# A graph layer on one core: part of the next tile's one-hots written ahead of the wait for a tile's sum, and gather landings counted in three blocks

## The chip, the core and the metric

The kernel runs on one core of a Trainium2 chip, as one program. The time is the device time of that core in microseconds, the median of several runs. The profile is of one execution; its own time stands beside its span, since the durations quoted come from it.

Engines are named as the profile names them: PE is TensorE's matmuls (PEld its weight loads), DVE VectorE, ACT ScalarE, POOL GpSimd, SP SyncE. DVEq, ACTq and so on are the sequencers of these engines, where register work and DMA issues run.

## What is computed

The input `x` has 6250 rows of 256. It is layer-normalised, then three things are added to it: a graph layer, a gated linear-attention layer, and after a second normalisation a feed-forward layer that acts on the half of the rows with the largest routing weight.

```python
h_sparse = _maxk(h_neigh, 32)                  # xn @ W_neigh, largest 32 of each row
msg = h_sparse[src]                            # 200000 edges, dst sorted
summed = jax.ops.segment_sum(msg, dst, num_segments=n)
neigh = summed / jnp.maximum(deg, 1.0)[:, None]
x = x + xn @ W_self + neigh + mix(xn)
x = x + ffn(layernorm(x))                      # for the rows that the router picks
```

The edges are sorted by destination, and low destinations have many more edges than high ones.

## The kernel before, in words

The rows are cut into 50 tiles of 125. A first part (to about 365 us) computes the sparse rows, split into two half-precision parts, and stores them in DRAM as `rows_d` (1 KB a row), and the statistics of the attention. The second part, about 77% of the time, is a hardware loop of five iterations with ten tiles (*positions* `s` = 0 to 9) unrolled in each. Tile `n = 10 i + s` is called by its number from 0 to 49 below.

**The sum of a tile.** Sorted edges are cut into groups of 512 (4 chunks of 128). For each group POOL issues four indirect gathers into `ring`, a ring of 8 groups (L600). SP waits for their landing, and counts it for PE in `s_landed` (L504). DVE writes the group's one-hot matrices (128 edges by 125 rows, four of them in one instruction, L1306) into `onehot`, a ring of `HOT` = 8 groups. PE multiplies: four matmuls of one-hot by rows (L954) and four small ones for the degree (L955). One such step on either engine is a *visit*. The last visit of a tile stands apart from the loops, since its group is shared with the next tile and isn't released. The limits of a tile, `g0` and `g1`, depend on the data: they are in the table `bounds` in SBUF, and each engine reads them into registers (`load`, L400), one tile ahead, at the end of the tile before (`look_ahead`).

**The dense tiles.** The five tiles with the most edges are not gathered. Their edges are counted by (source row, destination) in *windows*: DVE writes one-hots of pairs of chunks (L1331, L1337), PE multiplies them (L926), ACT copies the counts out (L726). Windows stand in positions 0 to 6 (`SHARE`: two in each of 0 to 5, one in 6). In positions 7 to 9 PE multiplies the counts with all rows of `rows_d`, in eight *pieces* (`from_rows`, L994). The pieces are loaded by ACT's queue (`load_h`, L696) into two buffers `hs`, 750 or 875 KB each; the first two when the last window has been copied out, each later one when PE has used the piece two before it. Position 9 has no gathered groups.

**The order inside a tile.** On PE: `ffn_down` (L905) and `ffn_up` (L898) of earlier tiles, `mix_hidden` (L864, which waits for DVE's `s_mix` of the tile before), `project`, `mix_open`, in positions 7 to 9 one piece, then `gathered`: the groups `g0` to `g1` cut into quarters or halves by `cut`, and between the cuts `turn_x3` (L890, the transpose of `x3`) and the windows or further pieces. The last matmul (L1031) signals `s_agg`. On DVE: the one-hots of visits and windows in the same order (`gathered`), then the rows of the attention and feed-forward results (L1382 to L1298), then the wait for `s_agg` (it ends at L1390), then the chain from the sum to `x2`, its normalisation, `x3` and the router weight (L1390 to L1433), each step waiting for the one before it. In ACT's stream the copy of the transposed `x3` (L684, it waits for `turn_x3`) stands ahead of the loads of the pieces.

All waits are on semaphores that count up. `s_step` is a set of 21 semaphores, one for each step of DVE's chain.

## Time and profile before

| | us |
|---|---|
| median of 3 runs | 2132.38 (2130.95 to 2132.94) |
| the profiled execution's own time | 2125.73 |
| its span | 2124.0, mean granted TensorE clock 0.854 |
| PE busy | 1572.6 (74% of the span) |
| DVE busy | 1250.0 (59%) |
| POOL busy | 1200.1 (57%) |
| ACT busy | 438.4 (21%) |

Busy shares are averages over stages with different limits. The waits and the order in time in the rows further below say which engine is waited for, and where.

### The profile page before, as it was taken

What the parts mean: (1) busy time and instruction counts of PE and PEld (TensorE: products, weight loads), DVE (VectorE), ACT (ScalarE), POOL (GpSimd) and SP (SyncE); (2) the same over time, 40 slices, a digit from 0 to 9 for tenths busy, and PEclk for the clock granted to TensorE, in tenths of its full rate; (3) what the DMA queues carried; (4) which work ended last, traced back from release to release, by engine and by line L of the source; (5) the groups of instructions that cost most, each with busy time, mean ns of one, the idle gap of its engine ahead of it and who ended that gap; (6) DMA issues with size and microseconds to landing.
All of it is one profiled execution on the core that took longest, in us unless ns stands there. A gap on an engine that the chain in (4) does not pass through costs nothing. (4 is left out here: it accounts for less than half of the span.)

```text
span 2124.0 us, 40110 instructions
## 1 busy us (share of the span) xinstructions
PE 1572.6 (74%) x8607; PEld 1132.7 (53%) x8608; DVE 1250.0 (59%) x3823; ACT 438.4 (21%) x974; POOL 1200.1 (57%) x1348
## 2 busy tenths in 40 slices
PE   2398554788778578888768888868898778887740
PEld 0154353355455456656656666656666566665630
DVE  5599973877566324666533766525666326663452
ACT  0254231011111112122112222112222122222200
POOL 1054544767777776777774777654676526664000
PEclk7699776888889788899987988889989889998865
DMA  4222114333343553334453433453333533335233
GB/s 134 75 84 72 58 45 127 90 95 108 108 118 110 153 178 110 110 109 118 139 175 111 116 104 113 143 153 87 92 111 109 158 100 106 96 96 149 68 107 117
DMA packets 149369, 236.37 MB, mean 111 GB/s; under 512 B 24807, under 2 KB 113859, under 8 KB 149219
## 3 DMA queue, kind: packets, MB, share of 16 engines
q0 software_dynamic: 52480, 142.82, 23.7%
q10 hardware_dynamic: 63586, 59.79, 9.3%
q1 hardware_dynamic: 33153, 31.95, 4.7%
q8 instruction: 71, 1.16, 0.2%
q14 instruction: 79, 0.65, 0.1%
HBM read 208.46 MB, written 26.01 MB: 110 GB/s over the span
## 5 line engine op out<-in xcount | busy, mean ns | idle before, releaser
L600 POOL DMA_INDIRECT ring<-rows_d,stage x1088 | 1075.8, 989 | 551.9 <-issue 303.6
L954 PE MATMUL bank<-ring,region_v 128*125 x1260 | 450.8, 469 | 90.5 <-SPq L504 45.3
L1306 DVE SCALAR_TENSOR_TENSOR region_v<-iota,tile_start,dstT 128x500 f16 x315 | 233.6, 742 | 189.5 <-issue 179.7
L954 PEld LDWEIGHTS bank<-ring,region_v 128*125 x1260 | 198.2, 157 | 241.2 <-issue 178.7
L926 PE MATMUL bank<-region_k 128*125 x622 | 214.4, 433 | 88.2 <-DVE region_k L1337 47.8
L1337 DVE TENSOR_SCALAR region_k<-iota,win_start,region_k 128x500 f16 x622 | 231.9, 414 | 1.2 <-issue 1.2
L905 PE MATMUL bank<-region_v 128*125 128x256 f32 x848 | 216.8, 413 | 16.6 <-issue 16.3
L955 PE MATMUL bank<-ones,region_v 128*125 128x2 f16 x1260 | 222.6, 177 | 0.0
L955 PEld LDWEIGHTS bank<-ones,region_v 128*125 x1260 | 201.3, 160 | 3.1 <-issue 2.5
L898 PEld LDWEIGHTS bank<-region_v 128*128 128x128 f32 x1664 | 196.6, 194 | 2.8
L1390 DVE TENSOR_SCALAR col_deg<-bank 125x1 f32<-125x1 f32 x50 | 7.9, 158 | 322.0 <-PE bank L1031 322.0
L898 PE MATMUL bank<-region_v 128*128 128x125 f32 x1664 | 196.8, 277 | 0.0
L905 PEld LDWEIGHTS bank<-region_v 128*125 128x125 f32 x848 | 170.1, 206 | 45.3 <-issue 17.1
L926 PEld LDWEIGHTS bank<-region_k 128*125 x622 | 85.0, 142 | 191.8 <-issue 185.0
L1331 DVE SCALAR_TENSOR_TENSOR region_k<-iota,region_k 128x250 f16 x311 | 131.4, 422 | 92.1 <-issue 66.1
L994 PE MATMUL bank<-region_k 125*125 125x512 f16 x250 | 84.4, 489 | 105.0 <-DMA region_k<-rows_d 105.0
L690 ACT ACTIVATE region_v<-bank,b 128x125 f32<-128x125 f32 x416 | 112.2, 381 | 113.3 <-PE bank L898 89.3
L726 ACT ACTIVATE region_k<-bank 125x500 f16<-125x500 f32 (+1 forms) x65 | 37.6, 579 | 381.9 <-PE bank L941 381.9
L690 ACT ACT_TABLE_LOAD x51 | 65.4, 1283 | 223.1 <-PE bank L905 137.4
L994 PEld LDWEIGHTS bank<-region_k 125*125 125x125 f16 x250 | 40.7, 174 | 130.5 <-DMA region_k<-rows_d 108.5
L573 POOL CAST region_r<-region_r 125x256 f16<-125x256 f32 x50 | 20.0, 399 | 150.9 <-DVE region_r L1210 149.3
L677 ACT ACT_TABLE_LOAD x51 | 65.4, 1283 | 188.3 <-PE bank L994 150.4
(284 smaller groups left out, 1968.3 us busy)
## 6 DMA issues: line engine op xcount, KB each, us to landing
region_k<-rows_d ACTq DMA_DIRECT2D x30, 750.0 KB
ring<-rows_d,stage POOLq DMA_INDIRECT x1088
region_k<-rows_d ACTq DMA_DIRECT2D x10, 875.0 KB
region_v<-xT_d ACTq DMA_DIRECT2D x53, 125.0 KB, 5.0
xT_d<-region_r ACTq DMA_DIRECT2D x51, 125.0 KB, 2.1
region_v<-in_x_dram SPq DMA_DIRECT2D x5, 1250.0 KB
rows_d<-region_r SPq DMA_DIRECT2D x50, 125.0 KB
region_k<-in_x_dram ACTq DMA_DIRECT2D x50, 125.0 KB
```

Source lines behind the costliest of these rows:

```text
L600: pool.indirect_dma_start(out=ring[:, c, :], out_offset=None, in_=rows_d, in_offset=bass.IndirectOffsetOnAxis(ap=stage[:, c:c + 1], axis=0 ...
L677: act.activation(hgT[0:GH, :], hg_pre, ACT.Gelu, bias=bg1[:, 0:1]).then_inc(s_hg, 1)
L690: last = act.activation(hidT[:, n, :], bank[(7, 4)[n // 4]][:, n % 4 * T:(n % 4 + 1) * T], ACT.Gelu_apprx_tanh, bias=b1[:, n:n + 1])
L898: m = pe.matmul(bank[(7, 4)[n // 4]][:, n % 4 * T:(n % 4 + 1) * T], w1[:, k, n * 128:(n + 1) * 128], x3T[:, k, :], start=(k == 0), stop=(k ...
L905: m = pe.matmul(out, hidT[:, n, :], w2[:, n, :], start=(n == 0), stop=(n == NH - 1))
L926: m = pe.matmul(out, lo_words[:, u * LW:(u + PAIR * (HOT_PAIRS - 1)) * LW + T][:, bass.ds(lo, T)], key_words[:, u * KEYS:(u + PAIR * (HOT_ ...
L954: m = pe.matmul(total, onehot_s, row_s, start=False, stop=False, skip_group_check=True)
L955: d = pe.matmul(deg_sum, onehot_s, ones16[:], start=False, stop=False, skip_group_check=True)
L994: m = pe.matmul(dense_sum, counts16[:, b, :], hs[:, q % 2, (b - first) * 2 * C:(b - first + 1) * 2 * C], start=False, stop=False, skip_gro ...
L1306: dve.scalar_tensor_tensor(out=hot_slots[:, bass.ds(hot, GC), :], in0=iota[:, 0:T].rearrange("p (a t) -> p a t", a=1).to_broadcast([128, G ...
L1331: dve.scalar_tensor_tensor(out=lo_hot[:, bass.ds(slot, PAIR), :], in0=iota[:, 0:T].rearrange("p (a t) -> p a t", a=1).to_broadcast([128, P ...
L1337: last = dve.tensor_scalar(key_words[:, u * KEYS:(u + PAIR * (HOT_PAIRS - 1) + 1) * KEYS][:, bass.ds(key, KEYS)], iota[:, 0:KEYS], win_fla ...
```

## The change

There are three parts. First, the first `LEAD` = 4 groups of a tile (or all up to `g1`, if there are fewer) get a limit of their own, `led`, in a new part of the table (`T_LEAD`). DVE writes their one-hots in the tile before, between the feed-forward rows and the wait for `s_agg` (`hot_ahead`). It does so for the first tile ahead of the loop, and not in position 8, since position 9 has no groups. On PE the visits of these groups come first, then `turn_x3`, and only then the rest; `cut` now cuts `led` to `g1`, without the first quarter, and the window or piece of each section comes ahead of its visits and not behind them. Second, `look_ahead` reads two values (`T_G1` and `T_LEAD`) where it read one, and on DVE it comes ahead of the wait. Third, the landings are counted in three sets of semaphores for blocks of 20, 20 and 10 passes over the edges (`s_land[block][q]`), and the steps of DVE's chain in 7 semaphores with three counts each. With the data of this run there is one pass: only block 0 runs, and the other two are jumped over behind it.

```diff
-    def __init__(self, engine, semaphores, count):
+    def __init__(self, engine, semaphores, counts):
     def mark(self, instruction):
-        instruction.then_inc(self.semaphores[self.n], 1)
+        instruction.then_inc(self.semaphores[self.n // len(self.counts)], 1)
+    def at(self, n):
+        return self.semaphores[n // len(self.counts)], self.counts[n % len(self.counts)]
...
     HOT = 8
+    LEAD = HOT // 2
+    BLOCKS = ((0, 20), (20, 20), (40, 10))
...
             def look_ahead(self, n, last):
                 if not last:
                     self.ahead = load(self.engine, n + 1 + T_G1)
+                    self.lead = load(self.engine, n + 1 + T_LEAD)
...
         def cut(engine, g0, g1, parts):
-            if not parts:
+            if parts < 2:
                 return [g0, g1]
             middle = engine.snap((g0 + g1) // 2)
-            first = [engine.snap((g0 + middle) // 2)] if parts > 1 else []
             last = [engine.snap((middle + g1) // 2)] if parts > 2 else []
-            return [g0] + first + [middle] + last + [g1]
+            return [g0, middle] + last + [g1]
```

On PE:

```diff
-                    cuts = cut(pe, g0, g1, len(parts) + len(sums))
+                    with pe.If(led > g0):
+                        with pe.Fori(g0, led) as g:
+                            visit(finals, g, True, total)
+                    if turn:
+                        turn_x3(one)
+                    cuts = cut(pe, led, g1, len(parts) + len(sums))
                     for at, (first, end) in enumerate(zip(cuts, cuts[1:])):
-                        with pe.If(end > first):
-                            with pe.Fori(first, end) as g:
-                                visit(finals, g, True, total)
-                        if turn and at == 0:
-                            turn_x3(one)
                         if at < len(parts):
                             count_window(i, *parts[at])
                         elif at < len(sums):
                             from_rows(sums[at])
+                        with pe.If(end > first):
+                            with pe.Fori(first, end) as g:
+                                visit(finals, g, True, total)
                     visit(finals, g1, False, total)
```

On DVE:

```diff
+            def hot_ahead(n, i, s):
+                if s == PER - 1:
+                    first, finals = load(dve, n + (T_G0 + 1)), load(dve, n + (T_VIS + 1))
+                    led = load(dve, n + (T_LEAD + 1))
+                else:
+                    first, finals, led = ends.end, ends.visits + (s + 1), ends.lead
+                with dve.If(led > first):
+                    with dve.Fori(first, led) as g:
+                        visit(finals, g, tile_after(i, s, 1))
...
-                    cuts = cut(dve, g0, g1, len(parts))
+                    cuts = cut(dve, led if s < PER - 1 else g0, g1, len(parts))
                     for at, (first, end) in enumerate(zip(cuts, cuts[1:])):
+                        if at < len(parts):
+                            window(i, *parts[at])
                         with dve.If(end > first):
                             with dve.Fori(first, end) as g:
                                 visit(finals, g, tile)
-                        if at < len(parts):
-                            window(i, *parts[at])
                     visit(finals, g1, tile)
...
-                st = Places(dve, s_step, one)
+                st = Places(dve, s_step, [dve.snap(n * 3 + u) for u in (1, 2, 3)])
...
                 ffn_rows(st, n, y_sum, yw[:, u, :], one)
+                ends.look_ahead(n, s == PER - 1)
+                if s != PER - 2:
+                    hot_ahead(n, i, s)
                 dve.wait_ge(s_agg, one)
...
-                st.after(a)
-                ends.look_ahead(n, s == PER - 1)
+                if s + 1 < PER and SHARE[s + 1] == 0:
+                    hold(dve, *st.at(a))
+                else:
+                    st.after(a)
```

In the first part of the program, where the table is made, and on SP (POOL's loops are changed in the same way):

```diff
+            dve.memset(bounds[:, T_LEAD + NT:T_LEAD + NT + 1], 0)
+            a = st.mark(dve.tensor_scalar(lead[:], bounds[:, T_G0:T_G0 + NT], float(LEAD), None, ALU.add))
+            st.after(a)
+            dve.tensor_tensor(bounds[:, T_LEAD:T_LEAD + NT], lead[:], bounds[:, T_G1:T_G1 + NT], ALU.min).then_inc(s_bounds, 1)
...
+            def landings(block, passes):
+                with sp.Fori(0, passes) as r:
+                    with sp.Fori(0, rounds) as j:
+                        for q in range(RING):
+                            sp.wait_ge(s_land[block][q], (r * ROUNDS + j + 1) * (16 * GC))
+                            sp.sem_inc(s_landed, 1)
+                            sp.sem_inc(s_restage, 1)
+
+            landings(0, passes)
+            with sp.If(general > 0):
+                for block in range(1, len(BLOCKS)):
+                    landings(block, BLOCKS[block][1])
```

**DVE, around its wait for the tile's sum (position 1).** L1306 is the last one-hot of the tile, L1382 to L1298 are the attention and feed-forward rows, and L1390 is the first instruction behind the wait for `s_agg`. Before:

```order
L1306 SCALAR_TENSOR_TENSOR region_v<-iota,tile_start,dstT 128x500
L1381 REGISTER_ALU
L1382 TENSOR_TENSOR region_k<-region_k,region_v 125x256
L1386 TENSOR_TENSOR region_k<-region_k,bank 125x256
L1296 TENSOR_TENSOR region_v<-bank,region_v 125x256
L1298 ISA
L1298 TENSOR_SCALAR region_v<-region_v,w_at 125x256
L1390 TENSOR_SCALAR col_deg<-bank 125x1
L1391 COPY region_v<-bank 125x256
```

After, L1334 is what was L1298 and L1444 what was L1390. These rows stand between the two; L408 is the reading of table values into registers, L1342 the one-hots of a group:

```order
L408 TENSOR_LOAD bounds
L408 ISA x3
L408 TENSOR_LOAD bounds
L408 ISA x2
L1404 COMPARE_AND_BRANCH
L1405 UNCONDITIONAL_BRANCH
L1405 ISA
L1342 ISA x3
L1342 SCALAR_TENSOR_TENSOR region_v<-iota,tile_start,dstT 128x500
L1405 REGISTER_ALU
L1405 COMPARE_AND_BRANCH
L1404 UNCONDITIONAL_BRANCH
```

Behind the wait there were no one-hots of groups until the chain was done; now up to four stand ahead of it, with two register loads in front.

**PE, at the end of a tile (position 1).** L1031 is the matmul that signals the tile's sum, L905 and L898 are the feed-forward matmuls that follow. Before:

```order
L1030 MATMUL bank<-zeros 125x2
L1031 MATMUL bank<-zeros 125x2
L400 ISA
L400 TENSOR_LOAD bounds
L400 ISA x2
L905 MATMUL bank<-region_v 125x256 x8
```

After, with L1061 for L1031, L932 for L905 and L925 for L898:

```order
L1060 MATMUL bank<-zeros 125x2
L1061 MATMUL bank<-zeros 125x2
L408 ISA
L408 TENSOR_LOAD bounds
L408 ISA x3
L408 TENSOR_LOAD bounds
L408 ISA x2
L932 MATMUL bank<-region_v 125x256 x8
```

A second register load now stands between the end of one tile and the first matmul of the next.

## Rows read from the trace of the kernel before

**Rows 1.** The longest waits of the whole execution: who waits for whom, total, times, longest.

```profile
DVE col_deg L1390 <- PE bank L1031: 322.0, 50, 25.2
...
PE bank L994 <- DMA region_k<-rows_d: 105.0, 14, 10.5
...
PE bank L926 <- DVE region_k L1337: 47.8, 102, 0.8
PE bank L954 <- SPq L504: 45.3, 17, 6.2
...
PE bank L954 <- DVE region_v L1306: 26.9, 50, 1.0
```

**Rows 2.** Timeline of DVE, sum of tile 21 to sum of tile 22: start, us, instruction [idle before, releaser].

```profile
1213.36 0.41 DVE L1290 SCALAR_TENSOR_TENSOR region_v<-region_v,bank 128x250 f32<-128x250 f32 x1
...
1218.82 0.20 DVE L1433 TENSOR_SCALAR w_at<-col_w,br 125x1 f32 x1
1220.98 0.74 DVE L1306 SCALAR_TENSOR_TENSOR region_v<-iota,tile_start,dstT 128x500 f16 x1 [1.96 <-issue]
1222.49 0.42 DVE L1331 SCALAR_TENSOR_TENSOR region_k<-iota,region_k 128x250 f16 x1 [0.77 <-issue]
...
1227.65 0.74 DVE L1306 SCALAR_TENSOR_TENSOR region_v<-iota,tile_start,dstT 128x500 f16 x1 [0.43 <-issue]
...
1236.29 1.60 DVE L1306 SCALAR_TENSOR_TENSOR region_v<-iota,tile_start,dstT 128x500 f16 x2 [0.27 <-issue]
...
1239.28 0.35 DVE L1298 TENSOR_SCALAR region_v<-region_v,w_at 125x256 f32<-125x256 f32 x1
1242.32 0.16 DVE L1390 TENSOR_SCALAR col_deg<-bank 125x1 f32<-125x1 f32 x1 [2.69 <-PE bank L1031]
```

**Rows 3.** L1390's waits in 1145:1334, 1447:1623 and 1735:1898: total, times.

```profile
  PE bank L1031: 15.6, 7
...
  PE bank L1031: 18.3, 7
...
  PE bank L1031: 13.3, 7
```

**Rows 4.** Register loads of DVE's sequencer, 1147 to 2005: ns min/median/max.

```profile
L400 DVEq TENSOR_LOAD <-bounds x78: 300/306/327, 1157.1 to 1993.4; - x78
```

**Rows 5.** Timeline of PE: the first matmuls behind the sum of tile 21.

```profile
1212.38 0.88 PE L905 MATMUL bank<-region_v 128*125 128x256 f32 x3 [0.16 <-issue]
```

**Rows 6.** Timeline of PE in tile 27 (position 7).

```profile
1354.49 3.69 PE L905 MATMUL bank<-region_v 128*125 128x256 f32 x16
...
1361.68 0.64 PE L864 MATMUL bank<-region_v,wg1g 128*64 128x125 f32 x4
...
1365.44 1.72 PE L994 MATMUL bank<-region_k 125*125 125x512 f16 x7
...
1368.18 0.41 PE L890 MATMUL bank<-ident,region_v 125*128 125x125 f32 x2
1374.86 3.25 PE L994 MATMUL bank<-region_k 125*125 125x512 f16 x7 [6.26 <-DMA region_k<-rows_d]
...
1387.67 2.82 PE L994 MATMUL bank<-region_k 125*125 125x512 f16 x6 [7.56 <-DMA region_k<-rows_d]
...
1396.25 0.20 PE L1030 MATMUL bank<-zeros 128*125 128x2 f16 x1
```

**Rows 7.** Timeline of ACT in tile 28 (position 8).

```profile
1410.24 0.38 ACT L684 ACTIVATE region_v<-bank 128x250 f32<-128x250 f32 x1 [4.41 <-PE bank L890]
1410.39 0.28 ACTq L696 DMA_DIRECT2D region_k<-rows_d  x1
```

**Rows 8.** Timeline of PE, tile 28, the piece loaded there.

```profile
1422.17 2.82 PE L994 MATMUL bank<-region_k 125*125 125x512 f16 x6 [9.61 <-DMA region_k<-rows_d]
```

**Rows 9.** POOL's waits for PE in 366:531 (tiles 0 to 2) and 817:930 (10 to 12).

```profile
POOL ring L600 <- PE bank L954: 31.2, 7, 18.5
...
POOL ring L600 <- PE bank L954: 15.3, 5, 10.7
```

100 lines of the change are left out of this document (56 added, 44 removed).

## The prediction

> **What bounds the kernel now.** I read the list of waits first. The reader is to see there that no engine waits for one thing alone: DVE waits for the sum of a tile at every one of the 50 tiles, 322.0 us in all, and PE waits for DVE in small bites (47.8 us for window one-hots, 26.9 us for those of groups), for SP's count of landings (45.3 us) and for the loaded pieces (105.0 us) [rows 1]. Then I laid the timeline out tile by tile. It shows three kinds of stretches.
>
> In the tiles with windows of the last three iterations PE and DVE are nearly level. DVE is idle at the sum only 15.6, 18.3 and 13.3 us over seven tiles each (position 9 and the six behind it) [rows 3], and PE's bites are spread over the same tiles. One tile shows the cycle: the sum of tile 21 is there at about 1212.2 (PE goes on at 1212.38 [rows 5]), DVE's chain ends with L1433 at 1218.8, the first one-hots of the next tile start at 1220.98 after 1.96 us of register work, the last rows (L1298) at 1239.28, and then DVE waits 2.69 us until 1242.32 [rows 2]. DVE works some 27 of 30 us, PE never sits idle for long, and each waits for the other once in a cycle.
>
> In positions 7 and 8 the pieces pace PE: 6.26 and 7.56 us of waiting in tile 27, 9.61 us in tile 28 [rows 6, 8].
>
> In the first two iterations the gathers pace everything. PE waits for SP there, and POOL loses time only where its ring is full. After the start of the first tile (18.5 us, which stays) that is 31.2 - 18.5 = 12.7 us in tiles 0 to 2; behind position 9 of the first iteration it is 15.3 us, of which one wait is 10.7 [rows 9].
>
> **The change part by part.**
>
> *One-hots ahead, in the window tiles.* No instruction of this work is removed: four visits of DVE move from behind the chain to ahead of the wait. What can be gained is DVE's idle time at the sum, 15.6 + 18.3 + 13.3 = 47.2 us in the last three iterations [rows 3]. It is filled completely, because the moved section is longer than any of these waits: two register loads and the set-up, about 2 us, then four visits at 0.74 + 0.27 us, some 5.8 us in all against a wait of 2.69 in the tile shown and 47.2 / 21 = 2.2 on average [rows 2, 3]. From then on DVE is the bound, and what counts is what the new order costs it. I count the gaps of one tile with six visits. Before: 1.96, 0.77, 0.43, 0.77, 0.43 and twice 0.27, together 4.9 us [rows 2]. After: 1.5 from the chain to the first window (one load, no group), 1.0 from window to window past an empty section, 0.43 and 0.27 to the last two groups, about 1.95 ahead of the leading section and three times 0.27 in it, together 6.0. So a tile costs DVE 1.1 us more. Over 18 tiles that is 20, and 47 - 20 = 27. PE can deliver that: its waits for DVE are 47.8 + 26.9 = 74.7 us over some 35 window tiles, 2.1 a tile or 38 over 18 [rows 1]. In the last iteration the cost eats the wait in single tiles, and what one tile has over isn't carried on; I take 3 off. Term: **-24**.
>
> The second load is the disputed price. A load takes 0.306 us on DVE's sequencer [rows 4]; with the operations around it I take 0.7 us, because a section with a load starts 0.77 us after a group's one-hots and one without 0.43 us, while most of the load runs beside the 0.74 us instruction ahead of it [rows 2]. The Trainium skill (DMA: Bandwidth & Descriptors, "Latency and other measured facts") gives a floor of about 600 ns for a `tensor_load`; the trace has half of that, and the trace decides. By the page each extra load would cost 0.3 us more, an estimate of 9 us over the tiles of this term and the loads on PE below.
>
> *The late chain.* DVE now reaches the sum up to 5.5 us late in a window tile. The cover is PE's feed-forward work: it starts at 1354.49 and the first matmul that needs the chain (L864, through `s_mix`) at 1361.68, 7.2 us later [rows 6]. The chain's `s_mix` comes about 1.6 us after its start (L1290 ends at 1213.77 [rows 2]), so 5.5 + 1.6 = 7.1: covered, with nothing to spare. I cost it at nothing. With the cover gone every microsecond counts in each tile where it happens. What is late next is `x3`, which PE needs only behind four visits.
>
> *Gathers.* PE releases four ring slots at once at the start of a tile, where it released one to three before a window. That takes away POOL's waits for a slot that is stuck behind a window. I take half of the 12.7 us in tiles 0 to 2 (the next window holds up a slot again) and, in tiles 10 to 12, the 15.3 - 10.7 = 4.6 us; the 10.7 us itself is the time to PE's first visit and stays [rows 9]. As POOL paces PE in both iterations, these pass to the end: **-11**. In those iterations the faster tiles otherwise only wait longer for landings.
>
> *Positions 6 to 8.* This speaks against the change. A visit takes 1.1 us at the full clock (L890 starts at 1368.18, the matmuls of the piece end about 1367.1 [rows 6]). In position 6 four visits instead of two stand ahead of the last window, so the first pieces are loaded 2.2 us later. In position 8 `turn_x3` moves behind three more visits, and ACT issues the load of the next piece right after the copy that waits for it (1410.24, then 1410.39) [rows 7]. PE waits for that load, so it lands 3 x 1.1 = 3.4 us later [rows 8]. Against that, fewer visits are left behind the last piece. In tile 27 the last piece runs from 1387.67 to about 1390.4, then four visits until 1396.25, 5.9 us, the first at half clock (after the wait the seven matmuls of a piece take 3.25 us where they took 1.72) [rows 6]. Two visits are left, about 3.9 us. So position 7 is level (+2.2 - 2.0), and position 8 loses 3.4 - 1.9 = 1.5, a little less with fewer groups. With 2.7 us for tiles 17 and 18 (both move with `turn_x3`; in tiles 7 and 8 the gathers cover it) and 4 for the last three iterations: **+7**.
>
> *PE's second register load.* The first matmul after a tile's sum already starts with a gap of 0.16 us [rows 5], so one load is just hidden behind the last visit and 0.7 us more is not. Where DVE or the gathers pace, this is covered; in positions 6, 8 and 9 of four iterations it isn't: 13 x 0.7, **+9**.
>
> *The rest.* Three short DVE operations and two waits for the table: **+1**. The three blocks of landings cost nothing in a run with one pass: the same waits and gathers run, and the jump over the other blocks comes when POOL has issued its last gather. The seven step semaphores change no order and hold as many waits.
>
> Sum: -24 - 11 + 7 + 9 + 1 = **-18 us**. The profiled execution took 2125.7 us, 6.7 below the median of the runs, so 2107.7 in its terms, and **2114 us** as a median.
>
> **The rivals.**
>
> *More is gained* (chance 0.17). For: the register work of the leading section may start while DVE's last rows run, and PE's load may find cover in the visits that now follow each other without waits. With DVE's extra at nothing (-20) and PE's loads free (-9) the time is 2114 - 29 = 2085; half of it 2099. Against: 1.96 us of exposed register work stands in every tile [rows 2].
>
> *Nothing is left* (0.14). The gathers are as late as before, since the next window holds the slots (+11), and the tiles with five groups gain nothing (+5): 2130. For: in an iteration paced by landings only POOL's own waits can be won, and I could place only half of them.
>
> *DVE's chain comes too late* (0.13, the other side). The place is PE's L864. If the leading section is longer than I think, or holds for a free one-hot slot, PE waits there and the cycle grows by the same amount. At 1.0 us more per tile the 18 tiles give back 18 us and the gain is gone; that is the point from which it decides. At 1.5 us more: +27, so 2141. For: the margin is 0.1 us. Against: the slot that the fourth leading one-hot needs was freed five visits before the end of the tile, and DVE was busy for only part of the cycle.
>
> My forecast has 0.56. It covers 2104 to 2124, and the two neighbours add 2094 below and 2134 above; beyond these I leave 2 in 10. About 0.2%, 4.3 us, is what a measurement of this kernel can tell from no change. Faster by more: the forecast, the larger gain and a third of the nothing-case, with some of the forecast lost, 0.74. Within: 0.13. Slower: 0.13.
>
> **What the profile of the changed kernel would show.** DVE's wait at the sum nearly gone in positions 0 to 5, left in 7 and 8. PE's waits for group one-hots near zero, those for window one-hots no smaller than before, since DVE is the bound. L1061 to L932 on PE 0.8 us apart instead of 0.4. POOL's waits for PE shorter in tiles 0 to 2. The load of the piece in position 8 some 17 us after the sum of the tile before instead of 14, and PE's wait for it as long as before, since PE comes later too. I am wrong if PE waits at `mix_hidden` for DVE, if the window tiles are more than 1.5 us a tile faster, or if POOL's waits are what they were.

## The result, and the profile after

| | before | changed |
|---|---|---|
| median of the runs beside each other | 2130.95 us (7 runs, 2122.79 to 2133.31) | 2144.22 us (7 runs, 2142.09 to 2152.93) |
| profiled execution, its span | 2125.73, 2124.0 us | 2152.93, 2151.2 us |
| mean granted clock of TensorE | 0.854 | 0.836 |

The ratio is 1.0076 [1.0053, 1.0099]: the change costs 0.76%, where a gain of 18 us, 0.8%, was forecast. The profiled execution of the changed kernel is the slowest of its seven and that of the kernel before lies 5 us under its median, so the two traces are 27 us apart and the medians 13. What follows splits up the 27, so about half of it lies in which executions were profiled, and not in the change.

The longest waits of PE in the changed kernel (who waits for whom, total, times, longest), to be read beside [rows 1]:

```profile
PE bank L1024 <- DMA region_k<-rows_d: 124.7, 16, 12.2
PE bank L953 <- issue: 63.5, 203, 0.7
...
PE bank L932 <- issue: 29.9, 15, 5.6
PE bank L981 <- SPq L517: 29.2, 11, 6.7
PE bank L953 <- DVE region_k L1373: 24.1, 57, 1.3
...
PE bank L960 <- ACT region_k L753: 15.0, 14, 1.2
...
PE bank L981 <- DVE region_v L1342: 11.9, 16, 3.7
```

The same view of the kernel before, from a second execution that was profiled among the experiments (before_here):

```profile
PE bank L926 <- DVE region_k L1337: 49.9, 107, 0.8
PE bank L954 <- SPq L504: 45.1, 17, 7.8
PE bank L926 <- issue: 37.7, 115, 0.6
PE bank L954 <- DVE region_v L1306: 28.3, 54, 0.7
...
PE bank L905 <- issue: 19.0, 6, 4.9
...
PE bank L933 <- issue: 9.3, 23, 0.8
```

The reader is to see an exchange of names. As waits for DVE the view has 36.0 us (24.1 + 11.9), not 78.2 (49.9 + 28.3). In return more stands under "issue", PE's own register work, in front of the matmuls of windows (L953, before L926) and of the feed-forward (L932, before L905). And 15.0 us stand at L960, the first matmul of a window (before, L933), which the view puts down to ACT. PE also waits 124.7 us for the pieces, not 105.0.

Such a label needs a second look. The view names whoever signalled last within the gap, also where PE's sequencer was busy with registers meanwhile. PE and ACT in tile 22:

```profile
1241.06 0.21 PE L960 MATMUL bank<-zeros 128*125 128x2 f16 x1 [1.10 <-ACT region_k L753]
```

```profile
1240.03 0.59 ACT L753 ACTIVATE region_k<-bank 125x500 f16<-125x500 f32 x1 [3.09 <-PE bank L968]
```

ACT copies the counts of the window just ended, but by the code the new window waits only for the copy of the one before that. PE's sequencer branches, loads a table value (0.30 us from 1240.31) and works on registers from 1239.8 to 1241.0: these 15 us are PE's own work too. The same holds for most of what is labelled as waiting for DVE. In the kernel before, the matmul at L926 has a gap of 0.33 us on average where the view names nobody (37.7 us, 115 times) and 0.47 where it names DVE (49.9 us, 107 times).

DVE's longest waits in the changed kernel:

```profile
DVE col_deg L1444 <- PE bank L1061: 225.6, 31, 23.1
...
DVE region_v L1342 <- issue: 154.3, 260, 2.7
...
DVE region_k L1433 <- DMA region_k<-in_x_dram: 133.9, 14, 19.8
...
DVE region_k L1367 <- issue: 110.8, 96, 8.6
```

The wait for the sum fell from 322.0 us in 50 tiles to 225.6 in 31 [rows 1]; it is mostly gone in the window tiles, as it was meant to be. One of them, tile 21 to 22, on DVE's timeline (start, us, instruction, idle before):

```profile
1226.49 0.20 DVE L1487 TENSOR_SCALAR w_at<-col_w,br 125x1 f32 x1
1228.07 0.43 DVE L1367 SCALAR_TENSOR_TENSOR region_k<-iota,region_k 128x250 f16 x1 [1.38 <-issue]
...
1233.97 0.42 DVE L1367 SCALAR_TENSOR_TENSOR region_k<-iota,region_k 128x250 f16 x1 [1.21 <-issue]
...
1239.39 1.61 DVE L1342 SCALAR_TENSOR_TENSOR region_v<-iota,tile_start,dstT 128x500 f16 x2 [0.84 <-issue]
...
1242.27 0.35 DVE L1334 TENSOR_SCALAR region_v<-region_v,w_at 125x256 f32<-125x256 f32 x1
1244.69 0.74 DVE L1342 SCALAR_TENSOR_TENSOR region_v<-iota,tile_start,dstT 128x500 f16 x1 [2.06 <-issue]
...
1250.41 0.16 DVE L1444 TENSOR_SCALAR col_deg<-bank 125x1 f32<-125x1 f32 x1 [1.89 <-PE bank L1061]
```

Four one-hots stand between 1244.69 and 1248.5, and DVE still waits 1.89 us for the sum, where it waited 2.69 [rows 2]: the sum itself comes later, 31.7 us behind the one before instead of 30.1. The starts of sections cost 1.38, 1.21, 0.84 and 2.06 us.

Where the time went shows best between two ends of a sum on PE (the last L1031 or L1061 of each tile). Added up by position over the five iterations (tile 0 left out), in us:

| kernel | positions 9 and 0 to 5 | 6 | 7 | 8 | 6 to 8 |
|---|---|---|---|---|---|
| before | 1060 | 141 | 193 | 176 | 510 |
| before_here | 1060 | 140 | 193 | 177 | 511 |
| changed | 1070 | 136 | 214 | 174 | 525 |

The two executions of the kernel before took nearly the same time (2125.73 and 2125.12 us), and their sums agree to 1 us. That isn't the scatter of one kernel: the seven runs of each kernel spread over 11 us. So the 10 us, and the 14 to 15, are those of this one execution of the changed kernel; the experiments below repeat their pattern in other traces. The rest of the 27: the first sum ends 3.4 us later, and half a microsecond comes back behind the last.

*The window tiles.* Four stretches from the sum of tile 8 to that of tile 15, 18 to 25, 28 to 35, 38 to 45. First the second execution of the kernel before, then the changed one (length, busy time of each engine, PE's granted clock, share of DMA, GB/s):

```profile
797.30:1021.00 223.70, 192.94 (x1114) 140.43 (x1114) 146.52 (x420) 47.49 (x103) 162.25 (x172) 0.91 0.39 111
1126.00:1332.60 206.60, 180.25 (x1036) 132.56 (x1036) 130.85 (x381) 47.49 (x103) 133.92 (x142) 0.89 0.37 104
1427.30:1619.80 192.50, 167.59 (x985) 125.66 (x985) 120.25 (x357) 47.49 (x103) 115.30 (x122) 0.90 0.34 99
1715.30:1898.40 183.10, 159.29 (x955) 120.50 (x955) 114.80 (x345) 47.49 (x103) 101.33 (x108) 0.93 0.33 93
```

```profile
798.00:1025.70 227.70, 196.42 (x1114) 142.06 (x1115) 150.44 (x424) 47.44 (x103) 165.24 (x175) 0.88 0.40 113
1127.60:1338.70 211.10, 183.17 (x1036) 135.27 (x1037) 132.48 (x384) 47.45 (x103) 135.16 (x143) 0.86 0.36 103
1438.80:1632.20 193.40, 171.53 (x985) 127.80 (x985) 121.73 (x361) 47.44 (x103) 110.74 (x117) 0.86 0.34 97
1731.50:1919.30 187.80, 163.84 (x954) 124.69 (x953) 116.55 (x349) 47.45 (x103) 95.88 (x101) 0.88 0.31 89
```

The same matmuls keep PE busy 715.0 us instead of 700.1, at a granted clock of 0.86 to 0.88 instead of 0.89 to 0.93. PE's idle time in these stretches, added up by what ended it: 53.1 us for DVE and 51.3 of "issue" before; 17.3 for DVE, 71.8 of "issue" and 15.0 at L960 in the changed kernel. So 36 us less under DVE's name stand against 36 more under the others: PE's idle time is the same, 105 us. How much of it PE really waited shows in the rows of its sequencer: before DVE's signal it had nothing to do for 10.7 of the 53.1 us before, and for 3.6 of the 17.3 after; at L960 for 0.4 of the 15.0. The rest is PE's own register work, before and after. The net loss is the longer busy time at a lower clock.

*Positions 7 and 8.* PE in tile 27 (position 7), then in tile 28, and ACT in tile 28:

```profile
1383.02 3.25 PE L1024 MATMUL bank<-region_k 125*125 125x512 f16 x7 [5.28 <-DMA region_k<-rows_d]
1397.68 2.82 PE L1024 MATMUL bank<-region_k 125*125 125x512 f16 x6 [11.42 <-DMA region_k<-rows_d]
```

```profile
1432.79 2.82 PE L1024 MATMUL bank<-region_k 125*125 125x512 f16 x6 [10.28 <-DMA region_k<-rows_d]
```

```profile
1421.24 0.38 ACT L711 ACTIVATE region_v<-bank 128x250 f32<-128x250 f32 x1 [6.74 <-PE bank L917]
1421.39 0.28 ACTq L723 DMA_DIRECT2D region_k<-rows_d  x1
```

In tile 28 the load goes out 17.2 us after the end of the sum (1404.2), PE waits 10.28 us where it waited 9.61 [rows 8], and the position is level. In tile 27 the piece in the middle starts 23.6 us after the end of the sum (1359.4) where it started 20.4 us after it (1354.5), and the last one costs 11.42 us of waiting where it cost 7.56 [rows 6].

ACT shows why tile 27 loses. Its sequencer issues a store and three small loads between the sum and the load of the middle piece, and the store's issue is long. First before_here (sum at 1353.6), then the changed kernel (1359.4):

```profile
1354.45 9.92 ACTq L739 DMA_DIRECT2D yw_d<-region_v  x1
...
1370.41 0.29 ACTq L696 DMA_DIRECT2D region_k<-rows_d  x1
```

```profile
1361.19 12.00 ACTq L766 DMA_DIRECT2D yw_d<-region_v  x1
...
1379.62 0.29 ACTq L723 DMA_DIRECT2D region_k<-rows_d  x1
```

The store goes out 0.9 us after the sum before and 1.7 with the change, and holds the sequencer 2 us longer. Ahead of it stand the loads of the first two pieces, the second of them issued 5.6 us ahead of the sum before and 2.8 us ahead of it with the change, since four visits now stand ahead of the last window (with two, in lead_2, it is 5.6 again). Tiles 37 and 47 show the same, so the load of the middle piece is late there because the first pieces are.

DVE's wait for the input rows (L1433) grew from 57.1 us in before_here to 133.9, and they come by the same queue. In tile 29 ACT issues a store and then that load, first in before_here, then in the changed kernel:

```profile
1428.22 0.30 ACTq L739 DMA_DIRECT2D yw_d<-region_v  x1
1428.62 0.59 ACTq L716 DMA_DIRECT2D region_k<-in_x_dram  x1
```

```profile
1439.74 5.72 ACTq L766 DMA_DIRECT2D yw_d<-region_v  x1
1445.55 1.32 ACTq L743 DMA_DIRECT2D region_k<-in_x_dram  x1
```

DVE has the rows at 1454.32, builds the next tile's one-hots behind them, and reads the sum of tile 29 at 1462.11, 5.5 us after it was there (1456.6). The four tiles of position 0 behind it took 160 us, where the kernel before has 148 and 152.

### The profile page after: what moved, and what is told of

The parts are those of the page before. It is cut to its first block and busy times, and to the rows that moved or that the text cites. A ratio compares the mean times of both kernels' runs of the same rounds, so it can differ in the third digit from the quotient of the medians.

```text
span 2151.2 us, 40690 instructions
## 1 busy us (share of the span) xinstructions
PE 1585.5 (74%) x8607; PEld 1143.3 (53%) x8608; DVE 1247.0 (58%) x3826; ACT 438.0 (20%) x974; POOL 1199.7 (56%) x1348
## 3 DMA queue, kind: packets, MB, share of 16 engines
q0 software_dynamic: 52480, 142.82, 23.6%
## 5 line engine op out<-in xcount | busy, mean ns | idle before, releaser
L981 PE MATMUL bank<-ring,region_v 128*125 x1260 | 429.9, 460 | 57.5 <-SPq L517 29.2
L1342 DVE SCALAR_TENSOR_TENSOR region_v<-iota,tile_start,dstT 128x500 f16 x315 | 233.8, 742 | 188.4 <-issue 154.3
L953 PE MATMUL bank<-region_k 128*125 x622 | 225.0, 455 | 88.5 <-issue 63.5
L932 PE MATMUL bank<-region_v 128*125 128x256 f32 x848 | 234.0, 437 | 30.0 <-issue 29.9
L932 PEld LDWEIGHTS bank<-region_v 128*125 128x125 f32 x848 | 182.8, 222 | 63.3 <-issue 31.3
L925 PEld LDWEIGHTS bank<-region_v 128*128 128x128 f32 x1664 | 196.2, 194 | 2.8
L925 PE MATMUL bank<-region_v 128*128 128x125 f32 x1664 | 196.4, 277 | 0.0
L953 PEld LDWEIGHTS bank<-region_k 128*125 x622 | 88.1, 145 | 197.9 <-issue 191.5
L1024 PE MATMUL bank<-region_k 125*125 125x512 f16 x250 | 83.9, 487 | 124.8 <-DMA region_k<-rows_d 124.7
L1444 DVE TENSOR_SCALAR col_deg<-bank 125x1 f32<-125x1 f32 x50 | 7.8, 156 | 225.6 <-PE bank L1061 225.6
```

The lines of the kernel that those rows point to most:

```text
L925: m = pe.matmul(bank[(7, 4)[n // 4]][:, n % 4 * T:(n % 4 + 1) * T], w1[:, k, n * 128:(n + 1) * 128], x3T[:, k, :], start=(k == 0), stop=(k ...
L932: m = pe.matmul(out, hidT[:, n, :], w2[:, n, :], start=(n == 0), stop=(n == NH - 1))
L953: m = pe.matmul(out, lo_words[:, u * LW:(u + PAIR * (HOT_PAIRS - 1)) * LW + T][:, bass.ds(lo, T)], key_words[:, u * KEYS:(u + PAIR * (HOT_ ...
L981: m = pe.matmul(total, onehot_s, row_s, start=False, stop=False, skip_group_check=True)
L1024: m = pe.matmul(dense_sum, counts16[:, b, :], hs[:, q % 2, (b - first) * 2 * C:(b - first + 1) * 2 * C], start=False, stop=False, skip_gro ...
L1342: dve.scalar_tensor_tensor(out=hot_slots[:, bass.ds(hot, GC), :], in0=iota[:, 0:T].rearrange("p (a t) -> p a t", a=1).to_broadcast([128, G ...
```

## The experiments

The first eight runs (no_lead to lead_6_8) fell on two chips on which the kernel before itself takes 2675 to 2676 us, not 2130. The last section says what is different there; their ratios aren't carried over to the first chip. The other ten, from before_here on, fell on three chips and ran beside a kernel before of 2126 to 2130 us.

Which positions build ahead, and which keep the order of before, is a table in all of these; the code of a position in OLD is that of the kernel before:

```diff
+    LEADS = (...)   # positions with a leading section
+    OLD = (...)     # positions in the order of the kernel before
...
-                if s != PER - 2:
+                if (s + 1) % PER in LEADS:
                     hot_ahead(n, i, s)
```

**no_lead**, and once more as **no_lead_2**: `LEADS = ()`, `OLD = 0..8`.

> The change without any one-hots ahead: no position has a leading section, and the order of visits, transpose, windows and pieces is that of the kernel before. What stays is the three blocks of landings, the seven step semaphores, the larger table and the second register load of look_ahead, ahead of the wait on DVE. If the cost is in the moved one-hots and the new order, this is within 0.2% of the kernel before. If it is in the added code and loads (the loop is entered 5.7 us later in the changed kernel's trace, and its loads stand at 50 tile ends), it is slower by 6 us or more, 0.3%.

> No one-hot is built ahead and every position has the order of the kernel before; what is left of the change is the three blocks of landings with their own semaphores, the rewritten counts and the loads of one more table. Both theories expect no change, 0.998 to 1.002. More than 1.003 would say that part of the loss comes from the blocks or from where the code lies, and not from the order of the work.

Measured, at 2675 us: 1.0031 [0.9998, 1.0064] and 1.0048 [1.0010, 1.0086], on the side of a small cost of the blocks and the longer tables, 0 to 0.9% there. On a chip of 2130 us they weren't run alone, so up to some tenths of the 0.76% may be theirs. One trace speaks against much of it: lead_6_8_b below has them too, and its positions 9 and 0 to 5 take the 1060 us of the kernel before.

**lead_1_8**: `LEADS = 1..8`, `OLD = 0`. **lead_1_5**: `LEADS = 1..5`, `OLD = 0, 6, 7, 8`. **turn_first**: all lead, and in positions 7 and 8

```diff
+                    if turn and s in TURN_FIRST:
+                        turn_x3(one)
                     with pe.If(led > g0):
                         with pe.Fori(g0, led) as g:
                             visit(finals, g, True, total)
-                    if turn:
+                    if turn and s not in TURN_FIRST:
                         turn_x3(one)
```

> The change without the leading section of position 0: DVE writes nothing ahead of the sum of position 9, and position 0 runs in the order of before. Theory 'one section too many': DVE is the bound from position 9 to 5, seven leading sections of about 6 us stand there against six savings, and the one at position 9 makes DVE late for the sum. Then this is 18 to 21 us faster than the changed kernel, 2123 to 2127 us, within 0.3% of before. Rival 'pieces': the loss is in positions 6 to 8 alone, and this stays at about 2144 us, 0.6% slower than before.

> Leading sections and the new order only in positions 1 to 5; positions 0, 6, 7 and 8 as before. Both theories have their cost taken away (about 20 us at position 9 and 0, about 15 to 20 us in positions 6 to 8), and only the window tiles are left, which gained about 5 us in the trace. Expected: 2115 to 2128 us, 0 to 0.7% faster than before. If it is slower than before, the leading section costs more than the idle time it fills in the window tiles too.

> The changed kernel with one thing moved: in positions 7 and 8 the transpose of x3 stands ahead of the four leading visits. Theory 'pieces': the late transpose holds back the load of the next piece by 3.4 us in position 8 (and in 7 of the second iteration). Then position 8 gets 3.4 us shorter in four iterations, 12 to 14 us in all: 2130 to 2133 us. Rival: only the first pieces (late by the visits ahead of the last window in position 6) and the gathers beside them matter, and this is 0 to 4 us faster than the changed kernel.

Measured, at 2675 us: 1.0122 [1.0075, 1.0169], 1.0229 [1.0180, 1.0278] and 1.0155 [1.0103, 1.0207]. The losses are larger than any theory had, and they don't order as either said. The traces show something else on such a chip (last section).

**whole** (the changed kernel again), **lead_0_5** (`LEADS = 0..5`, `OLD = 6, 7, 8`) and **lead_6_8** (`LEADS = 6..8`, `OLD = 0..5`).

> The changed kernel once more, unchanged, as the yardstick for the other three runs on this chip. Both theories expect what was measured before: slower than the kernel before by 0.5 to 1.0% (ratio 1.005 to 1.010) if this chip gives the kernel before some 2130 us. Should this chip be one on which the kernel before takes far longer than 2130 us, neither theory has a number for it.

> The one-hots are built ahead for positions 0 to 5 only; positions 6, 7 and 8 have the order of the kernel before on DVE and PE. Theory A (positions 6 to 8 carry half the loss: there the transpose and the issue of the pieces' loads come behind the leading visits, and DVE builds position 6's one-hots inside the stretch that it bounds): 10.4 us of the 28 between the two profiled executions lie between the sums of positions 5 and 9, and 4 leading one-hots fewer in the stretch from 9 to 5, so half of the loss goes: ratio 1.001 to 1.004. Theory B (the dearer starts of sections on DVE in positions 0 to 5 are the loss): it stays as it is for the whole change, 1.006 to 1.009.

> The one-hots are built ahead for positions 6, 7 and 8 only; positions 0 to 5 have the order of the kernel before. Theory A: the loss of positions 6 to 8 is there without anything of the rest: ratio 1.004 to 1.008. Theory B: nothing is left of the loss, 0.999 to 1.002.

Measured, at 2675 us: 1.0212 [1.0167, 1.0258], 1.0282 [1.0228, 1.0336] and 0.9999 [0.9964, 1.0034]. On such a chip the loss comes from building ahead in the window tiles, as far as the intervals tell.

**before_here** is the kernel before without an edit. **spaced** keeps GpSimd from issuing gathers back to back:

```diff
+                                if s % 2 == 1:
+                                    for k in range(4):
+                                        hold(pool, s_pad, g * 8 + s // 2 * 4 + k + 1)
+                                        pool.memset(pad[:], 0.0).then_inc(s_pad, 1)
```

> The kernel before, unchanged, for its own trace on the chip of the experiments. If that is again the chip on which it takes some 2675 us, both theories expect what the run with no one-hots ahead showed there: DVE and PE's sequencer have register and branch instructions of 0.6 to 1.4 us where the trace of the kernel before on the first chip has none over 0.25 us, some 190 on DVE and 250 on PE, nearly all while GpSimd issues gathers back to back. On a chip that gives 2130 us there are none.

> The changed kernel with four tiny memsets on GpSimd, each waited for, behind every second gather, so that gathers never come back to back for long; nothing else differs. Theory of the starved sequencers (on the slow chip PE and DVE get instructions at some 0.7 us for two, from about 7 us into a run of back-to-back gathers until it ends, and the change makes more such runs: 835 long register instructions on the two against some 450): the long ones fall below 300 and the time by 25 us or more, ratio to the kernel before at most 1.011. Rival (the long instructions have another cause, and gathers only come later): they stay above 700, and the time rises, ratio 1.02 to 1.05. On a chip of 2130 us both expect 1.005 to 1.02, the price of later gathers.

Measured: before_here 2125.12 us, one run; spaced 1.2122 [1.2091, 1.2152], beside a kernel before of 2129.55. The run fell on a chip of 2130 us, so spaced says nothing on the starved sequencers. It shows the price of later gathers: PE waits for SP's count of landings 434.0 us in all, where it waited 29.2 in the changed kernel. The expected 1.02 was far off.

**visits_first** puts each section ahead of the window piece (on PE also ahead of the dense piece), as in the kernel before, and keeps the leading one. DVE's wait for the last step of its chain is also written with `hold` in all positions now. On DVE:

```diff
-                        if at < len(parts):
-                            window(i, *parts[at])
                         with dve.If(end > first):
                             with dve.Fori(first, end) as g:
                                 visit(finals, g, tile)
+                        if at < len(parts):
+                            window(i, *parts[at])
```

**lead_2** is the changed kernel with `LEAD = HOT // 4`, two groups ahead instead of four.

> The changed kernel with its one-hots ahead, but in each section behind the leading one the groups stand ahead of the window piece again on PE and DVE, so that no two window pieces come back to back. Theory A (dearer starts: the first window behind a tile's chain begins 1.38 us after it and the second 1.2, where the kernel before had 1.96 and 0.79 for a visit and a window): DVE's idle labelled issue falls by 0.5 us a tile and more, and half of the change's loss goes: ratio 1.000 to 1.004 on a chip of 2130 us, 1.008 to 1.015 on one of 2675. Theory B (starved sequencers, decided by how gathers are bunched, which the leading section does): no difference from the whole change, 1.017 to 1.025 on the chip of 2675 us.

> The changed kernel with two groups' one-hots ahead in place of four. Theory A (what costs is the leading section in position 9, whose sum DVE had hardly waited for, and the seventh section in the stretch that DVE bounds, 5.7 us each with four groups): both halve, some 14 us over five iterations, while half of the filled waits come back: ratio 1.002 to 1.006 on a chip of 2130 us. Theory B (starved sequencers): fewer slots are let go in one burst, long register instructions fall from 835 to 550 to 700, ratio 1.008 to 1.016 on the chip of 2675 us. If only the number of sections counts, the size of the leading one changes nothing: 1.02 there.

Measured: visits_first 1.0085 [1.0061, 1.0109]. By PE's sums the window stretches are then level with the kernel before (807.0 us against 805.9, PE busy 699.6), and positions 6 to 8 take 534 us, 9 more than in the changed kernel; that the dense pieces now come behind the whole section is the likely reason, which no run separates. So the order behind the leading section moves some 13 us in the window tiles and gives nothing to the total, where Theory A expected 1.000 to 1.004. lead_2: 0.9968 [0.9949, 0.9987], the first that is faster than the kernel before. Theory A had it slower and was wrong; Theory B has no number for a chip of 2130 us. Its window stretches:

```profile
797.20:1022.10 224.90, 190.70 (x1113) 139.03 (x1113) 148.71 (x422) 47.43 (x103) 163.09 (x174) 0.92 0.39 112
1123.60:1327.20 203.60, 179.12 (x1036) 131.84 (x1035) 130.80 (x383) 47.43 (x103) 135.63 (x142) 0.88 0.37 106
1427.50:1616.70 189.20, 163.59 (x984) 123.51 (x983) 120.26 (x359) 47.44 (x103) 114.29 (x120) 0.93 0.34 99
1713.00:1897.20 184.20, 161.26 (x955) 122.05 (x954) 114.75 (x347) 47.43 (x103) 99.02 (x104) 0.89 0.32 92
```

They add up to 801.9 us, 18 less than with four. PE has 11.0 us of gaps there under DVE's name and 93.9 of "issue", 104.9 in all as in the kernel before (53.1 + 51.3 = 104.4); but it is busy 694.7 us, not 715.0.

**lead_0_5_b**, **lead_6_8_b** and **turn_first_b** are the kernels of those names once more, and **lead_2_0_5** is lead_0_5 with two groups ahead.

> Once more the one-hots ahead for positions 0 to 5 only, 6 to 8 in the order of the kernel before. Theory A (on a chip of 2130 us the whole loss stands in position 7, five tiles, 193 us before and 214 with the change, where the loads of the pieces are issued 3 to 4 us later behind the leading visits; positions 9 to 5 cost 10 us at most): the 20 us are gone, ratio 0.998 to 1.003. Theory B (the loss is spread over the starts of sections in positions 0 to 5): 1.005 to 1.009. On a chip of 2675 us both expect 1.02 to 1.03, as measured there.

> Once more the one-hots ahead for positions 6, 7 and 8 only, 0 to 5 in the order of the kernel before. Theory A: the loss of position 7 is there by itself, some 20 us less the 5 that position 6 gains: ratio 1.004 to 1.010. Theory B: 0.999 to 1.002. On a chip of 2675 us 0.997 to 1.003, as measured there.

> Once more the changed kernel with the transpose of x3 ahead of the leading visits in positions 7 and 8. Theory A: the loads of the pieces go out at the time of the kernel before (16.8 us after the sum in position 7, not 20.1; 13.9 in position 8, not 17.1), so position 7 gives back 12 us or more of its 21 and position 8 stays: ratio 0.998 to 1.003. Rival (the loads land late because gathers share their stretch, not because they are issued late): PE's waits for pieces stay above 120 us, and the ratio at 1.006 to 1.009. On a chip of 2675 us 1.012 to 1.020.

> Two groups' one-hots ahead in place of four, and only for positions 0 to 5; positions 6 to 8 have the order of the kernel before. Theory A: what two groups ahead gained (ratio 0.997), and the 7 us that position 7 still lost there besides (200 us against 193): ratio 0.992 to 0.996. Rival (what two groups ahead gained stands in positions 6 to 8 as well as in 0 to 5): 0.997 to 1.000. On a chip of 2675 us neither theory has a number; if the starved sequencers follow the leading visits there, 1.005 to 1.02.

**lead_1_8_b** is lead_1_8 once more; **lead_2_turn** has two groups ahead everywhere and the transpose first in positions 6, 7 and 8.

> Once more the changed kernel without the leading section for position 0 (in position 9 and ahead of the loop), position 0 in the order of the kernel before. Theory A (the section in position 9 is paid in full, since DVE had hardly waited for that sum: position 0's tiles took 160 us where two executions of the kernel before have 148 and 152, and the loop starts 3 us later): position 0 gives back 8 to 12 us, ratio 1.002 to 1.005. Rival (position 0's loss is the later return to the loop's start, not the section, and position 1 takes it instead): 1.006 to 1.009. On a chip of 2675 us 1.009 to 1.016.

> Two groups' one-hots ahead in all nine positions, and the transpose of x3 ahead of the leading visits in positions 6, 7 and 8. Theory A (the late issue of the loads of the pieces is what is left to lose with two groups: PE's waits for pieces 112.9 us against 103.6, position 7's tiles 200 us against 193): the waits fall to 97 to 105 us, and the gain of two groups ahead grows: ratio 0.991 to 0.996. Rival (with two groups the loads are late by 2 us only, which later waits take back): 0.995 to 0.999. On a chip of 2675 us no theory has a number below 1.0.

Measured beside kernels before of 2126.27 us (the four) and 2128.37 us (the last two), with the positions by PE's sums, each from the one execution that was profiled; lead_2 stands with them:

| kernel | ratio | 9 and 0 to 5 | 6 | 7 | 8 | 6 to 8 |
|---|---|---|---|---|---|---|
| lead_0_5_b | 1.0022 [1.0003, 1.0041] | 1066 | 139 | 203 | 171 | 513 |
| lead_6_8_b | 1.0031 [1.0013, 1.0048] | 1060 | 135 | 209 | 176 | 520 |
| turn_first_b | 1.0043 [1.0023, 1.0062] | 1073 | 144 | 200 | 166 | 511 |
| lead_1_8_b | 1.0066 [1.0041, 1.0091] | 1068 | 136 | 213 | 173 | 522 |
| lead_2_0_5 | 0.9978 [0.9960, 0.9996] | 1050 | 142 | 197 | 174 | 513 |
| lead_2 | 0.9968 [0.9949, 0.9987] | 1055 | 142 | 200 | 175 | 517 |
| lead_2_turn | 0.9946 [0.9927, 0.9964] | 1056 | 143 | 196 | 167 | 506 |

Both stretches lose by themselves, 0.22% and 0.31%, and together about as much as the whole change, within the intervals. Theory A had put the whole loss into position 7; theory B had none there. The 1.0022 lies in Theory A's range, the 1.0031 in neither. Neither stands alone. Position 7 loses 10 us in lead_0_5_b too, though it has the order of before; 8 of them are in tile 17 alone (45.2 us, not 37.0), where the first pieces were loaded 6.7 us ahead of the sum and not 12.6. By the ratios, the transpose ahead of the leading visits gives back a third of a per cent with four groups and 0.2 with two, but the intervals overlap in both pairs. Most of it is position 8 (174 to 166 us, 175 to 167), where the load now goes out 12.8 us after the sum. Positions 6 and 7 together go from 350 to 344 us, but in tile 27 of turn_first_b the load still goes out 20.4 us after the sum, so the mechanism held in one of its two positions. In tile 27 the transpose is done 14 us after the sum. By then ACT's sequencer has spent 12.27 us on the issue of its store, and it still has three small loads to issue: there the load didn't wait for the transpose. PE's waits for pieces, turn_first_b and then lead_2_turn:

```profile
PE bank L1051 <- DMA region_k<-rows_d: 96.6, 16, 12.5
```

```profile
PE bank L1051 <- DMA region_k<-rows_d: 94.9, 14, 11.0
```

The section in position 9 isn't the loss: without it (lead_1_8_b) position 0 gets back 8 us and positions 1 to 5 take 6 of them again, and the ratio hardly moves; the rival was right. lead_2_0_5 kept a gain of 0.22% where Theory A expected 0.4 to 0.8, so its rival was right; against lead_2 that is no difference that these runs can tell.

lead_2_turn is faster than both kernels: 2117.9 us against 2128.37, 0.54% under the kernel before. That lies in Theory A's range, but its interval reaches into the rival's too, and PE's waits for pieces fell below the 97 to 105 us expected.

## Why the prediction was wrong

The forecast was -18 us in the terms of the profiled execution, and the traces give +27 (the medians +13).

*One-hots ahead, -24: this is the step that failed.* The three window stretches of this term (from tile 18 on) take 592.3 us where before_here took 582.2: +10, so 34 of the 45 us between forecast and traces stand here. The filling itself about held: between the reads of the sum in the four window stretches DVE waits for it 16.5 us in 12 tiles, where it was 65.3 in all 28 (14.8 of the 47.2 us in the three that the term counts, not nothing). DVE's price was too low. Its gaps labelled "issue" went from 165.0 to 191.3 us, and those labelled as waits for PE to free a one-hot slot from 6.0 to 20.7, of which less than 1 us is waiting by the sequencer's rows. That is 41 us over 28 tiles, 1.5 a tile where 1.1 was forecast. Its wait for the input rows rose from 24.4 to 40.3, which was not priced.

What failed is the sentence "PE can deliver that". I read the gaps under DVE's name (47.8 + 26.9 us [rows 1]) as time that PE has to spare, 2.1 us a tile. By the rows of its sequencer PE waited for DVE 10.7 us in the 28 tiles, 0.4 a tile; the rest was its own register work, under DVE's name because DVE's signal fell into it. When the signal came earlier, the label went and the time stayed. lead_6_8_b shows this with the old order in positions 0 to 5: they take the same 805.8 us, but with 26.1 us for DVE and 74.3 of "issue". Over the eleven traces at 2130 us, spaced left out, PE's idle time in the four stretches is 101 to 115 us, whatever stands under DVE's name (9.8 to 53.1).

So filling DVE's wait was worth nothing, and PE's busy time grew by 15 us at a lower clock, which I hadn't priced. That growth comes back in every trace with four groups ahead of windows that come first: lead_0_5_b, turn_first_b and lead_1_8_b have 712.4, 724.0 and 707.3 us busy in stretches of 814.5, 824.6 and 815.9, beside 715.0 in 820.0. The seven others have 681.2 to 702.0 us busy in 796.1 to 807.0, with two groups ahead (694.7, 692.6, 681.2), with the old order behind the leading section (699.6) or with nothing ahead there (700.5, 700.1, 702.0). That it is the cost in the window tiles is shown; what makes the clock fall isn't: no run separates the length of a stretch without waits from the waits in it.

*Gathers, -11: right in kind, too large.* POOL's waits for PE in tiles 0 to 2, without the first long one, went from 12.7 to 8.4 us (the forecast wanted half of 12.7), and in tiles 10 to 12 from 4.6 to 1.0. But from the sum of tile 0 to that of tile 8 only 2.6 us came of it, and tiles 9 to 15 were 1.7 us slower (4.0 against before_here).

*Positions 6 to 8, +7: right in sign, half the size.* The traces have +14 to +15. Position 8 was priced at a loss of 1.5 and came out level; the load goes out 17.2 us after the sum, as worked out. Position 7 was to be level and lost 4.1 us in each iteration: the piece in the middle started 3.2 us later in tile 27, not 2.2, and the load that can go out only behind it took 11.4 us from its issue to PE's start, against 9.8 in before_here. The step that is missing is ACT's store: the first pieces, loaded later, stand ahead of it, and its longer issue holds back the next load.

*PE's second load, +9: the size is about seen, the place in part.* PE's gaps in front of L932 grew from 16.3 us (19.0 in before_here) to 29.9 in all. Behind position 6 the gap is 0.8 to 0.9 us in four iterations where there was none, as forecast. Behind position 8 there is only one, of 0.26 us. At the turn of the loop behind position 9 the four gaps are 19.5 us, where they were 13.1 and 15.8. The rest are one ahead of the loop (3.8, before 3.0), four of 0.3 to 0.8 in window tiles and one of 0.8 behind tile 0.

*The late chain, 0: right.* In the loop PE never waits for DVE at L891; one wait of 0.9 us stands ahead of it in both kernels. *The rest, +1:* the first sum ends 3.4 us later.

None of the three signs of being wrong came, and no rival had this outcome. One row of the expected profile would have told: PE's waits for window one-hots were to be "no smaller than before, since DVE is the bound", and they halved, from 47.8 to 24.1 us. The nearest in time, 2141 us by a late chain of DVE, needed the wait at L891. PE's room in the window tiles was misread, and a price for the clock was missing from the forecast and its rivals alike.

The Trainium skill's figure for a `tensor_load` (DMA: Bandwidth & Descriptors, "Latency and other measured facts"), about 600 ns at least, would have added an estimated 9 us, as the prediction says. DVE's and PE's loads have a median of 303 to 306 ns in the changed kernel too, so that isn't the missing part.

## What to carry to other kernels

Before you count a wait for another engine as room, look at what the waiting engine's own sequencer does in it. Compare the mean gap under the other's name with the mean gap of the same instruction that nobody is named for: here 0.47 us against 0.33, so most of the wait was the engine's own register work, and filling it gained nothing. Ask of a moved section what it stands ahead of on the queue that issues loads, and try it at half size: here two groups ahead gained 0.3% where four lost 0.8%. The transpose ahead of it gave 7 to 8 us in position 8, where a load waited for it, and little in position 7, where the load waited for a store's issue. Compare traces between two ends of the same sum by position, and use more than one execution of each kernel: two of the kernel before agreed to 1 us, but its runs spread over 11.

## What the runs showed of the hardware

On two of the chips the kernel before takes 2675 us instead of 2130. DVE's instructions last as long there (a group's one-hots have a median of 740 ns in before_here and in no_lead), and so do the 4 KB packets of the gathers' queue (226 ns on average in both), but many register instructions of the sequencers last longer. Here DVE's, in before_here and in no_lead (ns min/median/max):

```profile
L1306 DVEq FUSED_REGOPS  x945: 64/133/234, 351.6 to 1968.0; - x189
```

```profile
L1369 DVEq FUSED_REGOPS  x945: 2/133/1395, 364.4 to 2523.8; - x189
```

The long ones in a burst take some 0.7 us each, as if the instructions came late; that reason isn't shown. Counting register and branch instructions that last over 0.35 us more than is usual on their line: none on DVE in before_here and 3 on PE; 189 on DVE and 267 on PE in no_lead; 367 and 468 in whole. They come in bursts on both engines at the same time, while GpSimd issues gathers one behind the other. GpSimd and DVE in one tile of whole:

```profile
1576.99 0.94 POOL L633 DMA_INDIRECT ring<-rows_d,stage  x1 [9.90 <-PE bank L992]
...
1596.84 0.94 POOL L633 DMA_INDIRECT ring<-rows_d,stage  x1 [0.30 <-issue]
```

```profile
1581.84 0.72 DVE L1400 TENSOR_SCALAR region_k<-iota,win_start,region_k 128x500 f16 x2
1586.96 0.74 DVE L1369 SCALAR_TENSOR_TENSOR region_v<-iota,tile_start,dstT 128x500 f16 x1 [4.40 <-issue]
1589.88 0.74 DVE L1369 SCALAR_TENSOR_TENSOR region_v<-iota,tile_start,dstT 128x500 f16 x1 [2.18 <-issue]
```

The burst begins 4.9 us after GpSimd resumed (the first long instruction at 1581.90) and ends some 2 us behind the last gather of its run. A visit that takes 1 us takes 2.9 in it. Over the eight runs at 2675 us the counts and the ratios go together: 451 to 481 long instructions in no_lead, no_lead_2 and lead_6_8, with ratios up to 1.005, and 782 to 835 in the five others, with 1.012 to 1.028. The kernel before has no trace on such a chip. On a chip of 2130 us much longer runs of gathers than these have none (one of 204 in before_here, with no pause of 0.7 us in it). Why chips differ in this, and whether the gathers cause the bursts or only share them, is open: the run that was to tell (spaced) fell on the other kind of chip.
